# A perceiver block on one core: rotated keys made four steps ahead, the exponentials of two steps side by side, and a new order on TensorE, VectorE and GpSimd

## The reference

```python
ctx = layer_norm(context, ln_ctx_g, ln_ctx_b)        # 16 batches x 1024 x 256
kv = ctx @ Wkv                                       # 16 heads of 64
k = apply_rope(k, cos, sin)
attn = einsum('bhnd,bhsd->bhns', q, k) * 64 ** -0.5  # 64 latents against 1024 keys
attn = clip(attn, -11.0, 11.0)
attn = softmax(attn, axis=-1)
out = einsum('bhns,bhsd->bhnd', attn, v)
```

## Time and profile before

| | us |
|---|---|
| median of three runs | 1274.48 |
| profiled execution | 1269.03 |
| its span, first to last instruction | 1267.3 |
| PE busy | 1187.5 (94%) |
| DVE busy | 1040.4 (82%) |
| POOL busy | 695.0 (55%) |
| ACT busy | 661.3 (52%) |

### The profile page before, as it was taken

The page is one execution under the profiler, slowest core; times in us unless marked ns, Lnnn a source line. Parts: engine busy times, 40 slices in busy tenths (PEclk is TensorE's granted clock), DMA queues, the critical chain, the costliest instruction groups (busy, mean ns, idle before and its releaser), DMA issues.

```text
span 1267.3 us, 39950 instructions
## 1 busy us (share of the span) xinstructions
PE 1187.5 (94%) x16268; PEld 999.2 (79%) x16268; DVE 1040.4 (82%) x1954; ACT 661.3 (52%) x1089; POOL 695.0 (55%) x611
## 2 busy tenths in 40 slices
PE   7898999999999999999999999999999999999997
PEld 3687777878778777877777877777878788789997
DVE  6899987988978988988998988888877356668886
ACT  7664555555545555555455554555534233356664
POOL 3566666666656656666666655675454123333433
PEclk8999999999999999999999999999999999999999
DMA  6365555565555555655555555555554351556662
GB/s 225 84 168 148 135 131 132 141 151 146 144 131 146 142 147 138 150 131 131 137 145 146 148 136 146 131 132 140 155 124 114 111 192 36 184 173 194 203 185 72
DMA packets 136174, 181.36 MB, mean 143 GB/s; under 512 B 30316, under 2 KB 96312, under 8 KB 135864
## 3 DMA queue, kind: packets, MB, share of 16 engines
q1 hardware_dynamic: 110552, 150.80, 44.2%
q10 hardware_dynamic: 21360, 23.80, 7.1%
q0 software_dynamic: 4080, 4.22, 1.6%
HBM read 81.93 MB, written 30.56 MB: 89 GB/s over the span
## 4 chain that ended last, share of the span: by engine, by line
PE 44%; DVE 26%; DMA 8%; issue 8%; SPq 5%; POOL 4%; ACT 3%; POOLq 0%; DVEq 0%; ACTq 0%
PE bank L1526 12%; DVE p_lo L1073 7%; PE bank L1555 7%; PE bank L1882 6%; PE bank L1512 5%; DMA ksw<-kw 4%; DVE kr L1085 3%; DVE kw L1084 3%; SPq L452 3%; PE bank L1684 2%; DMA l_rows<-l_parts 2%; DVE shift L1030 2%; DVE pr L1052 2%; DVE kr_third L1085 2%; PE bank L1578 2%
## 5 line engine op out<-in xcount | busy, mean ns | idle before, releaser
L1526 PE MATMUL bank<-ct,wk_hi 128*128 128x512 f32 x1024 | 326.5, 400 | 4.5 <-DVE ct L1090 1.4
L592 POOL TENSOR_TENSOR kr<-kr,ksw 128x1024 f32<-128x1024 f32 x86 | 208.7, 2427 | 219.6 <-DMA ksw<-kw 144.0
L1555 PE MATMUL bank<-p_hi,xc 128*128 128x512 f32 x1024 | 315.8, 390 | 0.0
L1526 PEld LDWEIGHTS bank<-ct,wk_hi 128*128 128x128 f32 x1024 | 188.9, 190 | 47.1 <-issue 2.9
L1084 DVE TENSOR_TENSOR kw<-bank,stab 128x512 f32<-128x512 f32 x256 | 175.6, 686 | 59.3 <-PE bank L1526 49.1
L1555 PEld LDWEIGHTS bank<-p_hi,xc 128*128 128x128 f32 x1024 | 191.8, 188 | 39.7
L778 ACT ACTIVATE pr<-bank 128x1024 f32<-128x1024 f32 x128 | 131.4, 1027 | 171.1 <-DVE p_lo L1073 136.7
L1073 DVE TENSOR_TENSOR p_lo<-pr,p_hi 128x1024 fp32r<-128x1024 f32 x128 | 213.5, 1668 | 3.4 <-ACT p_hi L786 3.4
L1526 PE MATMUL bank<-ct,wk_lo 128*128 128x512 f32 x512 | 201.0, 393 | 0.0
L1555 PE MATMUL bank<-p_lo,xc 128*128 128x512 f32 x512 | 199.2, 389 | 0.0
L592 POOL TENSOR_TENSOR kr_third<-kr_third,ksw 128x1024 f32<-128x1024 f32 x42 | 102.7, 2445 | 112.9 <-DMA ksw<-kw 75.7
(11 more groups left out here) (223 smaller groups left out, 1895.7 us busy)
## 6 DMA issues: line engine op xcount, KB each, us to landing
ksw<-kw SPq DMA_DIRECT2D x512, 128.0 KB, 2.4
x_turned<-xt SPq DMA_DIRECT2D x120, 128.0 KB
ct_read<-x_turned SPq DMA_DIRECT2D x30, 512.0 KB
w_two<-in_L_ffn_W_dram SPq DMA_DIRECT2D x15, 1024.0 KB, 5.1
raw<-in_ctx_dram ACTq DMA_DIRECT2D x56, 256.0 KB, 3.2
x_slots<-fill ACTq DMA_DIRECT2D x32, 258.0 KB, 3.4
w_all<-in_L_ffn_W_dram SPq DMA_DIRECT2D x4, 2048.0 KB, 17.0
wo<-in_L_ffn_W_dram SPq DMA_DIRECT2D x7, 1024.0 KB, 4.9
```

The lines of the kernel that those rows point to most:

```text
L592: pool.tensor_tensor(kr_at(j + 2), kr_at(j + 2), ksw[:, i], ALU.add).then_inc(kr_done, 1)
L1526: last = pe.matmul(psK[:, a * 512:(a + 1) * 512], l[:, k, w], ct[:, h % 3, r, k], start=(m == 0), stop=(m == len(parts) - 1))
L1555: last = pe.matmul(psZ[c], xc[:, slot_, l, t, cols], r[:, i, :, t], start=(f == 0 and m == 0), stop=(f == 1 and m == len(parts) - 1), skip ...
```

## The change

- The keys are made four steps ahead instead of three, with a fourth buffer (`kr_fourth`).
- `pr` gets a slot for every step of two pairs, in the memory of `p_lo`, so the low part is written over the exponential. The exponential of step j no longer waits for a low part, but for the sums that read this slot last.
- PE's pair is now scores, scores, outputs (where due), sums, keys, sums, keys. Before, it was outputs, scores, scores, keys, sums, keys, sums.
- DVE's pair is one function. It clamps both steps, takes the first low part, and then runs `shifts` and `counted` of the second step. Only then does it turn the keys of step j + 4, and after the second low part those of step j + 5. Before, each step had shifts, counted, clamp, keys, low part.
- ACT takes both exponentials first, then each high part, normalised row and rounded row.
- POOL's add in an even step waits for the first half of the keys of step j + 4 (`k_ps`) in place of the clamp.
- SP issues the swap ahead of two small loads. The work that ends cross-attention (weights turned for the next layer, head projections) is placed anew around the last four steps.

The core of the diff, with the parts on constants and on the last steps left out:

```diff
@@ POOL, step(j)
                     if j >= 0:
-                        pool.wait_ge(clamp_done, j + 1)
+                        if there(j + 4) and j % 2 == 0:
+                            pool.wait_ge(k_ps, 2 * (j + 4) + 1)
+                        else:
+                            pool.wait_ge(clamp_done, j + 1)
                     pool.wait_ge(sw_ld[i], ((j + 2) // 2 + 1) * 64)
                     pool.tensor_tensor(kr_at(j + 2), kr_at(j + 2), ksw[:, i], ALU.add).then_inc(kr_done, 1)
...
@@ ACT
+            def exponential(j):
+                act.wait_ge(s_ps, j + 1)
+                wait(act, z_ps, j // 2 * 2 - 2)
+                act.activation(step_part(pr, j).rearrange("p (t h c) -> p h t c", h=2, c=P),
+                               heads[j % 2].rearrange("p h (t c) -> p h t c", c=P), ACT.Exp, scale=SCALE).then_inc(exp_done, 1)
...
@@ DVE
             def keys_turned(j, a):
-                if there(j + 3):
-                    i, f = (j + 3) % 2, (j + 3) % 4 // 2
+                if there(j + 4):
+                    i, f = j % 2, j % 4 // 2
...
-                    dve.wait_ge(k_ps, 2 * (j + 3) + a + 1)
+                    dve.wait_ge(k_ps, 2 * (j + 4) + a + 1)
                     if a == 0:
-                        wait(dve, kr_done, j + 2)
+                        if j >= -2:
+                            dve.wait_ge(sw_ld[i], 64 * ((j + 2) // 2 + 1))
...
+            def two_steps(j):
+                shifts(j)
+                counted(j)
+                clamped(j)
+                clamped(j + 1)
+                if due(j, 8):
+                    added((j - 8) // 4)
+                weights_low(j)
+                blocks_turned(j)
+                if due(j, 10):
+                    divided((j - 10) // 4)
+                if due(j + 1, 7):
+                    inverted((j - 6) // 4)
+                shifts(j + 1)
+                counted(j + 1)
+                keys_turned(j, 0)
+                keys_turned(j, 1)
+                weights_low(j + 1)
+                blocks_turned(j + 1)
+                if half_written(j - 1):
+                    half_low(half_written(j - 1))
+                keys_turned(j + 1, 0)
+                keys_turned(j + 1, 1)
...
@@ PE
             def outputs(n):
...
-                    pe.wait_ge(ku_done, 8 * n + 22)
+                    pe.wait_ge(ku_done, 8 * n + 24)
...
             def two_steps(j):
+                scores(j)
+                scores(j + 1)
                 if due(j, 8):
                     outputs((j - 8) // 4)
-                scores(j)
-                scores(j + 1)
-                if due(j, 8) and there(j + 3):
+                sums(j - 2)
+                if due(j, 8):
                     pe.wait_ge(o_sum, (j - 8) // 2 + 2)
-                keys(j + 3)
-                sums(j - 2)
                 keys(j + 4)
                 sums(j - 1)
+                keys(j + 5)
```

More of the change, by code:

```diff
@@ L439, in step @@
                     sp.dma_start(l_parts[:], zt[P - 1:P, KC - 1].rearrange("o (p e) -> o p e", e=4)).then_inc(lsum_ld, 16)
+                if there(j + 4):
+                    i = j % 2
+                    sp.wait_ge(kw_done, 2 * (j + 5))
+                    wait(sp, kr_done, j + 3)
+                    for r in range(4):
+                        to, of = r * HALF, (r ^ 1) * HALF
+                        sp.dma_start(ksw[to:to + HALF, i], kw[of:of + HALF, i]).then_inc(sw_ld[i], 16)
+                if due(j, 7):
+                    n = (j - 7) // 4
+                    sp.wait_ge(o_sum, 2 * n + 1)
+                    sp.dma_start(l_rows.rearrange("q h (p e) -> (q h p) e", e=4), l_parts[:]).then_inc(lsum_ld, 16)
+                if h:
+                    sp.wait_ge(xt_moved, 80 * (h - 2) + 64)
+                    if h >= 3:
+                        sp.wait_ge(k_ps, 2 * last_key(h - 3) + 2)
+                    sp.dma_start(low_as_read(h), x_turned.rearrange("c p s -> p c s")).then_inc(xt_moved, 16)
                 if due(j, 8):
@@ L445, in step @@
                         sp.dma_start(lsum[h_ * DH:(h_ + 1) * DH, :].rearrange("p (q c) -> p q c", q=2), l_rows[:, h_].partition_broadcast(DH)).then_inc(lsum_ld, 16)
-                if there(j + 3):
[L447 to L463, removed]
+            for j in range(-4, 0):
                 step(j)
@@ L884, in turned @@
                 act.copy(xnT[:, t % 2].rearrange("p k c -> p (k c)"), bank[:, 5, 0:D]).then_inc(xnT_done, 1)
-            for j in range(2, STEPS + 5):
-                step(j)
-                if j == STEPS + 1:
+            for j in range(2, STEPS + 6, 2):
+                even_step(j)
+                odd_step(j + 1)
+                if j == STEPS:
                     turned(0)
@@ L1144, in _ @@
             key_weights(1)
-            for j in range(-9, -3):
+            for j in range(-9, -4):
                 opening(j)
-                if -7 <= j <= -4:
+                if j >= -7:
                     latents_low(j + 7)
+            latents_low(3)
             query_weights_low(0)
             dve.wait_ge(tab_done, 2)
+            opening(-4)
             opening(-3)
+            query_weights_low(1)
             opening(-2)
-            query_weights_low(1)
             opening(-1)
@@ L1268, in constants @@
                                              op0=ALU.mult, op1=ALU.add)
-            for j in range(STEPS):
-                step(j)
+            for j in range(0, STEPS, 2):
+                two_steps(j)
                 if j == 2:
@@ L1281, in _ @@
                     value_weights(1)
-                if STEPS - 6 <= j < STEPS:
-                    t = j - STEPS + 6
-                    if t == 0:
+                if j >= STEPS - 6:
+                    if j == STEPS - 6:
                         dve.wait_ge(bo_ld, 32)
                         dve.wait_ge(x2_ld, 32)
-                    for u in (t, t + 6) if t < 2 else (t,):
-                        dve.tensor_tensor(raw[:, 0, u], raw[:, 0, u], bo_all[:], ALU.add).then_inc(xbo_done, 1)
+                    i = (j - STEPS + 6) // 2
+                    for t in range(3 * i, min(3 * i + 3, TT)):
+                        dve.tensor_tensor(raw[:, 0, t], raw[:, 0, t], bo_all[:], ALU.add).then_inc(xbo_done, 1)
             dve.wait_ge(xbo_done, TT)
@@ L1645, in _ @@
             queries(2, 1)
+            keys(3)
             queries(3, 1)
@@ L1651, in _ @@
             scores(1)
-            keys(3)
+            keys(4)
             queries(4, 1)
             queries(5, 1)
-            keys(4)
+            keys(5)
             queries(6, 1)
@@ L1697, in _ @@
                 two_steps(j)
-            outputs(QUADS - 3)
             scores(STEPS - 4)
             scores(STEPS - 3)
+            outputs(QUADS - 3)
             pe.wait_ge(o_sum, 2 * QUADS - 4)
-            keys(STEPS - 1)
-            sums(STEPS - 6)
-            pe.wait_ge(ku_done, 2 * STEPS)
             pe.wait_ge(vec2_ld, 32)
@@ L1721, in _ @@
             project_heads(0, 0, PAIRS)
+            sums(STEPS - 3)
             outputs(QUADS - 2)
```

132 lines of the change are left out of this document (67 added, 65 removed).

## The result

| | median us (range) | ratio to before (95% interval) |
|---|---|---|
| before, four runs | 1275.10 (1269.0 to 1280.7) | |
| changed, four runs | 1601.27 (1599.3 to 1604.31) | 1.2561 (1.25 to 1.2623) |

What follows compares the result with a forecast made beforehand. PE was taken to set the pace, DVE following at 88%. From 1269.0 us, 121 us for a ring of waits was added and 26.6 us of removed waits subtracted: forecast 1363 us, 7% slower, range 1310 to 1415 us.

Steps and rivals of the forecast that it cites:

- The ring: Circular waits: POOL's add and `rstd`, DVE's shift and turned keys, PE's keys; 1.99 us in 61 pairs, 121 us.
- The values chosen for `ve` and for the shift: Two instruction times in the ring, on POOL and DVE, chosen between ends: `ve` 0.19 us, shift 0.68 us.
- Everything else has room in a pair of 15.1 us.: Outside the ring nothing would delay a pair: DVE has 12.9 us of work, low part and POOL's add in time.
- Against it: 1.89 us did nothing. 8%.: Rival: PE's clock also falls behind the ring's waits; 104 us more if in every pair, 1467 us; chance 8%.
- The rival's own term for half of the pairs: PE's clock falling behind the ring's wait in only half of the pairs: 1415 us in all.
- I count the 6.8 us as gone too.: PE's output waits for DVE's turned keys and freed banks, 6.8 us, would go as outputs come behind the scores.
- The 18.1 us of waits for POOL's add: PE's score waits for POOL's add, 18.1 us, would go with the keys made four steps ahead.
- 'Issue' stays in full.: PE's score waits with "issue" as releaser, 25.2 us, would remain, as matmul count and small-matmul run don't change.
- The second rival: The ring costs less: shift not held by `xc` (-33 us), "issue" waits fall away (-25 us); 1305 us, chance 10%.
- The opening, "where I count it at nothing (within 5 us either way": One pair of key blocks moves from the end to the opening, counted at nothing; twelve matmuls are 2.72 us.
- Against it: the order of POOL and of DVE after the change: Argument against the no-ring rival, chance 6%: on POOL and DVE the waiting instruction stands in front.
- the rival in which the change does what the removed waits say: No ring: only the removed waits count, 26.6 us off 1269.0, so 1242 us, faster than before; chance 6%.

Runs made afterwards that it cites:

- e13: Changed kernel with one DVE reordering, the odd step's turned keys ahead of the transposes; late moves and POOL's wait for keys stay: 1440.98 us, ratio 1.1348.
- e2: Changed kernel with SP's four moves of the turned context blocks issued a step earlier; POOL's add still waits for the keys: 1409.04 us, ratio 1.1034.
- e8: e5 with the changed kernel's wait of POOL's add for the keys put back: 1427.31 us, ratio 1.1294.
- e5: Changed kernel with POOL's add waiting for the clamp, SP's moves a step earlier and the turned half's load ahead of the swap: 1280.22 us, ratio 1.0125.
- e12: e9 with the last two query projections ahead of keys 5 on PE, and DVE's odd-step turned keys ahead of the transposes: 1265.52 us, ratio 0.9958.
- e9: Changed kernel with POOL's add on the clamp, moves earlier, ACT's high part first, and the opening's shift ahead of turned keys: 1271.62 us, ratio 1.0039.

## Why the prediction was wrong, point by point

- **The ring, "61 x 1.99 = 121 us."** Right, mechanism and size: 117.0 us of waits, and the parts of the ring within 0.1 us. The values chosen for `ve` and for the shift were those that came.
- **"Everything else has room in a pair of 15.1 us."** This step failed, and it is the largest error. I added up each engine's work and two deadlines and did not follow SP's queue in the new order. The table of releasers before shows no sign of danger there, since the transposes waited only some 9 us for the moves in all. SP issued the moves behind a swap before as well. But the change has DVE turn the keys of that swap late in the pair, and puts the transpose, which waits for the moves, ahead of the keys that the outputs need. Both orders can be read off the code. It cost 132 us of waits, shown by e13 and e2; with the clock behind them taking the moves early gives 194 us.
- **"Against it: 1.89 us did nothing. 8%."** Two single waits in the rows before were taken as a rule for a wait that comes back in each pair. The same trace had more to say. Nine waits of 1.85 us or more stand in its steps, and behind three of them the granted clock was 0.50 for 3.4 us: behind that of 2.86 us and behind those of 2.20 and 2.39 here. Behind that of 2.46 it stayed at 1.00:

```profile
350.02 0.35 PE L1512 MATMUL bank<-qo,kr_third 64*64 64x64 f32 x9 [2.20 <-issue]
...
774.55 0.64 PE L1512 MATMUL bank<-qo,kr 64*64 64x64 f32 x28 [2.46 <-POOL kr L592]
...
804.38 0.92 PE L1512 MATMUL bank<-qo,kr 64*64 64x64 f32 x24 [2.39 <-POOL kr L592]
```

So the trace already had the clock fall behind waits little longer than 1.99 us, and the 8% left them out. PE's busy time grew by 115.6 us. From kernel to kernel, 52.4 go with the moves (changed to e2), 47.1 with the ring (e8 to e5), and 16.4 are left in e5 over before; e2 and e8 lie 0.3 apart. The rival's own term for half of the pairs, 52 us, was about the ring's.
- **"I count the 6.8 us as gone too."** The 18.1 us of waits for POOL's add went. The outputs' waits did not: 132.4 us in place of 6.8, by the step above; in the repaired order of e12 they are gone.
- **"'Issue' stays in full."** It did not: 25.2 us before scores became 0.3 there and 7.3 before outputs, one of them 6.5 us long. The second rival had these waits fall away while PE stands, and the other runs don't bear that reason out: e8, in which PE stands in every pair, has 20.6 us of "issue" before outputs, and e9, in which it hardly stands, 5.9. In every kernel of the new order they have left the scores for the outputs; their cause stays open.
- **The opening, "where I count it at nothing (within 5 us either way".** Scores start 12.4 us later. The keys that moved there are part of it; the shift of step -2, which the change put behind turned keys, is the rest, and with it PE's waits (7.3 against 1.4 us) and a slow clock (two stretches of 3.4 us at 0.50 between 49 and 60 us, none there before). e9 gives back 0.008, 10 us. That I had not read the opening's order on DVE is the same mistake as on SP, smaller.
- **"Against it: the order of POOL and of DVE after the change"**, on the rival in which the change does what the removed waits say. Right: only with the ring, the moves, the high part, the opening and the turned keys all put right (e12) does the change come out ahead, by 5 us and not 27.

Together: 117.0 + 132.4 + 10.6 us (the small groups) of waits, less the 50.8 of before, 115.6 of clock and 5.9 in the opening are 330.7, against 330.3 between the two spans (a few us of waits in neither list are left out). The forecast had 121 of these; the terms of its sum give 1363.4 as they are printed, not 1363.7, which changes nothing. That the direction came out right is not luck: with the ring alone e8 is 0.129 slower than before.

## What to carry to other kernels

Where a change reorders several engines, write down for each of them, the DMA-issuing one included, what stands behind every waiting instruction, and close each loop: three costs here (shift, transpose, the load's product) were an instruction that TensorE did not need yet, waiting in front of one on which it hung. A wait that comes back in every pair is priced with the clock behind it, not by one instance in a trace where such waits are rare. And when a wait is late because of a transfer, ask first what can be moved out from behind it; e13 got back 154 us with the transfer left where it stands in its queue.

## What the runs showed of the hardware

Waits of some 2 us on TensorE, one in each pair of 15 to 16 us with dense matmuls between them, had the granted clock at 0.50 behind nearly half of them (e8: 27 of 60 waits between 1.7 and 2.4 us; 32 stretches, 109.2 us in all). One small two-input product on VectorE takes 0.37 to 0.43 us in 31 of its 32 instances before. In the changed kernel 19 of the 32 take 2.26 to 2.31 us. Each of the 19 starts while a GpSimd add runs, and ends 0.28 or 0.29 us behind it; here the add had started 0.67 us earlier:

```profile
620.43 2.66 POOL L597 TENSOR_TENSOR kr_third<-kr_third,ksw 128x1024 f32<-128x1024 f32 x1 [6.62 <-PE bank L1561]
```

```profile
621.10 2.27 DVE L1090 TENSOR_TENSOR qo<-o_part,lsum 128x256 f32<-128x256 f32 x1
```

The Trainium skill, "SBUF — State Buffer", section "Who interferes with whom", has it that such a product and a GpSimd instruction share a read port, and that the one issued first keeps it. The add here was first and the product waited; the rows agree.
